# Four moves at the changeover of a two-layer block: the last chunk's root, the first routing weights' transposes, the shared expert's slice, and GpSimd's first product

## The reference

```python
xn = _layernorm(x)
x = x + L1_attn(xn) + L1_ffn(xn)
# L1_attn: q, k, v of the same token; for each token position a softmax over the 8 batch entries
attn = softmax(einsum('nqd,nkd->nqk', q, k) * scale)
out = einsum('nqk,nkd->nqd', attn, v) @ out_w.T + out_b
# L1_ffn: 16 experts of width 64, and a shared one of width 128
scores = sigmoid(x @ w_gate.T)
# groups of 4 experts; the 2 groups with the highest sum of their 2 best; then the 4 best experts
w = top4 / (sum(top4) + 1e-06)
combine = one_hot(idx) * w
routed = sum over e of combine[e] * (silu(x @ w1[e].T) * (x @ w3[e].T)) @ w2[e].T
shared = (silu(x @ w1_s.T) * (x @ w3_s.T)) @ w2_s.T
```

## Time and profile before

| | |
|---|---|
| median of 3 runs | 369.76 us (369.0 to 370.84) |
| profiled execution | 369.26 us |
| its span | 367.4 us |
| VectorE busy | 316.3 us, 86% |
| TensorE busy | 304.5 us, 83% |
| GpSimd busy | 238.8 us, 65% |
| ScalarE busy | 186.2 us, 51% |

### The profile page before, as it was taken

One profiled execution on the slowest core, in us unless ns is written; L12 is line 12 of the kernel. 1 busy time (PEld: TensorE's weight loads), 2 busy tenths in 40 slices (PEclk: granted clock), 3 DMA queues, 4 the chain that ended last, 5 costly groups with the idle time before them and its releaser, 6 DMA issues.

```text
span 367.4 us, 4905 instructions
## 1 busy us (share of the span) xinstructions
PE 304.5 (83%) x1371; PEld 218.4 (59%) x1371; DVE 316.3 (86%) x828; ACT 186.2 (51%) x505; POOL 238.8 (65%) x152
## 2 busy tenths in 40 slices
PE   0559777989889876773998988999999999899994
PEld 0336655868768665652654665765656666575662
DVE  5997899987987859837999999899898989989792
ACT  3346676866878586570253523635335362353611
POOL 3176487573745720142789679889898898988661
PEclk9978999999999999697999999999999999999999
DMA  4690000000000000008843324434333253324000
GB/s 137 176 271 1 2 0 1 3 1 2 1 1 2 0 1 2 0 14 160 186 113 57 96 79 101 100 87 129 110 91 117 58 140 87 115 83 118 3 29 29
DMA packets 21311, 24.81 MB, mean 68 GB/s; under 512 B 2428, under 2 KB 12068, under 8 KB 21284
## 3 DMA queue, kind: packets, MB, share of 16 engines
q1 hardware_dynamic: 20336, 24.09, 25.2%
q10 hardware_dynamic: 820, 0.39, 0.4%
q0 software_dynamic: 128, 0.01, 0.0%
HBM read 22.13 MB, written 2.36 MB: 67 GB/s over the span
## 4 chain that ended last, share of the span: by engine, by line
DVE 37%; PE 30%; issue 12%; POOL 8%; ACT 7%; DMA 3%; SPq 1%; ACTq 0%; DVEq 0%; POOLq 0%
PE Q L901 13%; PE VN L901 8%; PE T L901 5%; POOL prod_qk L841 5%; DVE att L1529 4%; DVE hid L1566 4%; DVE sgc L1553 3%; DVE rope_b L1305 3%; DVE rope_a L1303 3%; PE T L897 3%; POOL prod_pv L851 2%; DVE attn L1335 2%; ACT L735 1%; DVE xT_lo L1356 1%; DMA cw<-comb_table 1%
## 5 line engine op out<-in xcount | busy, mean ns | idle before, releaser
L841 POOL TENSOR_TENSOR prod_qk<-qkv 128x1024 f32<-128x1024 f32 x32 | 76.1, 2389 | 21.6 <-ACT qkv L551 12.4
L851 POOL TENSOR_TENSOR prod_pv<-prob,qkv 128x1024 f32<-128x1024 f32 x32 | 69.4, 2187 | 16.7 <-DVE att L1529 15.1
L901 PE MATMUL VN<-hid,w 128*128 128x512 f32 x144 | 74.6, 599 | 0.9 <-DVE hid L1566 0.9
L901 PE MATMUL Q<-xT_hi,w_hi 128*128 128x512 f32 x72 | 52.0, 722 | 1.2 <-issue 0.7
L1566 DVE TENSOR_TENSOR hid<-T,sgc 128x512 f32<-128x512 f32 x64 | 43.5, 680 | 0.0
L1515 DVE TENSOR_REDUCE scr<-prod_qk 128x128 f32<-128x1024 f32 x32 | 38.8, 1213 | 4.5 <-POOL prod_qk L841 4.3
L901 PE MATMUL Q<-bias,ones 128*128 128x400 f32 (+1 forms) x64 | 29.4, 459 | 15.2 <-ACT v_ext L629 7.1
L901 PE MATMUL T<-xT_hi,w_hi 128*128 128x512 f32 x72 | 30.5, 424 | 13.1 <-DVE hid L1566 13.0
L735 ACT ACTIVATE VN<-Q 128x512 f32<-128x512 f32 x32 | 18.6, 582 | 40.1 <-PE Q L901 26.5
L1529 DVE TENSOR_REDUCE att<-prod_pv 128x128 f32<-128x1024 f32 x32 | 38.3, 1198 | 0.0
L735 ACT ACTIVATE ND<-Q 128x512 f32<-128x512 f32 x32 | 18.6, 582 | 35.1 <-PE Q L901 32.2
(11 more groups left out here) (173 smaller groups left out, 761.8 us busy)
## 6 DMA issues: line engine op xcount, KB each, us to landing
cw<-comb_table SPq DMA_DIRECT2D x64, 256.0 KB, 4.5
out_x<-fin SPq DMA_DIRECT2D x8, 256.0 KB, 4.5
x<-in_x SPq DMA_DIRECT2D x2, 256.0 KB, 2.9
wraw<-in_w1T SPq DMA_DIRECT2D x1, 512.0 KB, 4.2
w3raw<-in_w3T SPq DMA_DIRECT2D x1, 512.0 KB, 4.7
w<-in_w2T SPq DMA_DIRECT2D x1, 512.0 KB, 5.8
rope_s<-in_c_sin ACTq DMA_DIRECT2D x1, 256.0 KB, 5.0
rope_c<-in_c_cos SPq DMA_DIRECT2D x1, 256.0 KB, 5.5
```

The costliest lines, as they stand in the source:

```text
L841: pool.tensor_tensor(prod_qk[:, t % 2], bc(qkv2[:, TH * half + t, j, 0:D], 1, NB), qkv2[:, :, j, D:2 * D], ALU.mult).then_inc(qk_prod, 1)
L851: pool.tensor_tensor(prod_pv[:, t % 2].rearrange("p (h e) b -> p b h e", e=HD), bc(prob[:, t].rearrange("p h b -> p b h"), 3, HD), qkv2[:, ...
L901: return pe.matmul(o, lhsT, rhs, start=start, stop=stop)
```

## The change

**The last chunk's root.** In step 9 the four layer-1 copies: ScalarE copies tile 0, and takes tiles 1 to 3 only behind the roots of step 10. The Sqrt table is loaded behind the copy `attnT` instead of ahead of it. VectorE's `route_masked` and `route_top` of half 0 move from step 9 to step 10, behind `plus_ffn`, and the first part of `route_chosen` behind `rms_values` of step 10.

**The first weights' transposes** stand ahead of chunk 7's tiles on TensorE, their copy ahead of the tiles' copies on ScalarE, followed by a two-element Sigmoid.

**Shared slice first.** The shared expert is slice 0 of each slot; routed slices are 1 to 8 (`routed_slice(s)` is s - 1, and w1, w3 and w2 are addressed by it). TensorE begins slot 0 when 31 of 32 tiles are kept.

**GpSimd's first product** waits until VectorE has done `route_above` of half 1 (`r_step` 16).

The diff:

```diff
--- before.py
+++ after.py
@@ -404,6 +404,8 @@
         NSLICE = NSLOT * NS
         BASE = (5, 14, 23, 31, 40, 48, 57, 65)
         LAST = BASE[NSLOT - 1] + 15
+        R_ROUTE = 13
+        R_ABOVE = R_ROUTE + 3
         COMB_AT = BASE[0] + 15
 
         def comb_bank(h):
@@ -413,6 +415,10 @@
 
 
             return (n + s) % 2
+
+        def routed_slice(s):
+
+            return s - 1
 
         def place(n):
 
@@ -660,6 +666,9 @@
                 if i == 1:
                     xnT_evac(0)
                 norms_rooted(i)
+                if i == STEPS - 2:
+                    for j in range(1, NJ):
+                        l1_tile(j)(i - 5)
                 if i == 3:
                     vu_norm()
                 if i > 1:
@@ -682,14 +691,17 @@
                 run(i, 4, xn2T_hi_evac)
                 if at(i, STEPS - 3):
                     sigmoid(0)
-                    act.activation(vu_n[:, 0, :], vu_n[:, 0, :], ACT.Sqrt)
                 run(i, 1, qkv_tile(2))
                 run(i, 2, attnT_evac)
+                if at(i, STEPS - 3):
+                    act.activation(vu_n[:, 0, :], vu_n[:, 0, :], ACT.Sqrt)
                 if i == STEPS - 2:
                     return
                 run(i, 1, qkv_tile(3))
                 run(i, 4, l1_tile(0))
                 run(i, 2, out_squares)
+                if i == STEPS - 3:
+                    return
                 run(i, 4, l1_tile(1))
                 run_end(i, 4, l1_tile(2))
                 run_end(i, 4, l1_tile(3))
@@ -712,11 +724,10 @@
                 l1_tile(2)(NB - 2)
                 l1_tile(3)(NB - 2)
                 xn2T_hi_evac(NB - 1)
-                l1_tile(0)(NB - 1)
-                l1_tile(1)(NB - 1)
                 combT_evac(0)
-                l1_tile(2)(NB - 1)
-                l1_tile(3)(NB - 1)
+                act.activation(vu_n[:, 0, :], vu_n[:, 0, :], ACT.Sigmoid)
+                for j in range(NJ):
+                    l1_tile(j)(NB - 1)
 
             pipeline(act, step, last_step)
 
@@ -727,11 +738,11 @@
             def gate(n, s):
                 act.wait_ge(g_ps, NS * n + s + 1)
 
-                if s >= 2:
-                    act.wait_ge(sgc_ready, (NS - 1) * n + s - 1)
+                if s >= 3:
+                    act.wait_ge(sgc_ready, (NS - 1) * n + s - 2)
                 else:
                     after(act, hid_ready, NS * n + s - 1)
-                gated = SB[side(n, s)] if s < NS - 1 else sg
+                gated = SB[side(n, s)] if s > 0 else sg
                 act.activation(gated[:, :], QB[side(n, s)][:, :], ACT.Silu).then_inc(sg_ready, 1)
 
             def attT_evac(u):
@@ -855,6 +866,7 @@
                         ALU.mult).then_inc(pv_prod, 1)
 
             pool.wait_ge(l1_kept, NT)
+            pool.wait_ge(r_step, R_ABOVE)
             for t in range(TH):
                 product_qk(0, t, 0, 0)
 
@@ -1039,12 +1051,12 @@
                 run(i, 1, qkv_tile(2))
                 run(i, 1, qkv_tile(3))
                 run(i, 2, attn_transposes(i))
+                if at(i, STEPS - 1):
+                    comb_transposes(0)
                 run(i, 2, ffn_product)
                 run(i, 4, l1_tile(0))
                 run(i, 2, output_product)
                 run(i, 4, l1_tile(1))
-                if at(i, STEPS - 1):
-                    comb_transposes(0)
                 run_end(i, 4, l1_tile(2))
                 run_end(i, 4, l1_tile(3))
                 if at(i, 1):
@@ -1058,7 +1070,7 @@
             pe.wait_ge(xn2T_lo, NB)
 
             pe.wait_ge(combT_ready, 1)
-            pe.wait_ge(l1_kept, NT)
+            pe.wait_ge(l1_kept, NT - 1)
             pe.wait_ge(w1_ready, 1)
             pe.wait_ge(w3_ready, 1)
             pe.wait_ge(ld_w2, 64)
@@ -1071,7 +1083,7 @@
                 pe.wait_ge(hid_ready, NS * n + s + 1)
                 if s == 0:
                     after(pe, yT_ready, n)
-                mm(VK[:, :], w2[:, s, :], hid[:, s % 3, :], s == 0, s == NS - 1).then_inc(y_ps, 1)
+                mm(VK[:, :], w2[:, routed_slice(s) % NS, :], hid[:, s % 3, :], s == 0, s == NS - 1).then_inc(y_ps, 1)
 
             def down_two_before(n, s):
 
@@ -1100,7 +1112,10 @@
                 j, half = place(n)
                 hi = xT_hi[:, TH * half:TH * half + TH, j, :]
                 lo = xT_lo[:, TH * half:TH * half + TH, j, :]
-                w = slice(s * P, (s + 1) * P)
+                at = routed_slice(s) % NS
+                w = slice(at * P, (at + 1) * P)
+                if n == 0 and s == 1:
+                    pe.wait_ge(l1_kept, NT)
 
                 after(pe, sg_ready, NS * n + s - 1)
                 g = QB[side(n, s)]
@@ -1398,6 +1413,8 @@
                     if g < NG - 1:
                         a = V.tensor_tensor(above[:, :, g, g + 1:NG], gv[:, :, g + 1:NG], own(NG - 1 - g), ALU.is_gt)
                 step_of(a)
+                if h == 1:
+                    assert r_done[0] == R_ABOVE
 
             def route_limits(h):
 
@@ -1472,7 +1489,8 @@
                 run(i, 2, head_blocks)
                 run(i, 3, plus_ffn)
                 if at(i, STEPS - 2):
-                    route_chosen(0, 0)
+                    route_masked(0)
+                    route_top(0)
                 if at(i, STEPS - 1):
                     route_chosen(0, 1)
                     route_weights(0)
@@ -1499,9 +1517,8 @@
                     route_limits(0)
                 if before_last(i):
                     rms_values(i)
-                if at(i, STEPS - 3):
-                    route_masked(0)
-                    route_top(0)
+                if at(i, STEPS - 2):
+                    route_chosen(0, 0)
                 if at(i, 1):
                     vu_sum()
 
@@ -1546,23 +1563,24 @@
 
             def weighted(n, s, k):
 
-                if s < NS - 1:
+                if s > 0:
+                    r = routed_slice(s)
                     dve.wait_ge(sg_ready, NS * n + s + 1)
-                    if s % 2 == 0:
-                        dve.wait_ge(ld_cw[s // 2], 32 * (n + 1))
-                    V.tensor_tensor(sgc[:, k, :], SB[k][:, :], cw[:, s // 2, s % 2, :], ALU.mult)\
+                    if r % 2 == 0:
+                        dve.wait_ge(ld_cw[r // 2], 32 * (n + 1))
+                    V.tensor_tensor(sgc[:, k, :], SB[k][:, :], cw[:, r // 2, r % 2, :], ALU.mult)\
                         .then_inc(sgc_ready, 1)
 
             def hidden(n, s, k):
 
-                if s < NS - 1:
-                    dve.wait_ge(sgc_ready, (NS - 1) * n + s + 1)
+                if s > 0:
+                    dve.wait_ge(sgc_ready, (NS - 1) * n + s)
                 else:
                     dve.wait_ge(sg_ready, NS * n + s + 1)
                 dve.wait_ge(u_ps, NS * n + s + 1)
 
                 after(dve, y_ps, NS * n + s - 2)
-                src = sgc[:, k, :] if s < NS - 1 else sg[:, :]
+                src = sgc[:, k, :] if s > 0 else sg[:, :]
                 V.tensor_tensor(hid[:, s % 3, :], UB[k][:, :], src, ALU.mult)\
                     .then_inc(hid_ready, 1)
```

## The result

The changed kernel takes 364.74 us (median of 4 runs, 364.25 to 365.62) against 369.69 us (4 runs, 369.00 to 370.84) for the kernel before on the same chip: ratio 0.9866, 95% interval 0.9834 to 0.9898, which is 4.95 us or 1.3% faster. Forecast: 365.1. Two of the later executions of the kernel before were far off (1048.70 and 1670.61 us) and are left out everywhere. The changed kernel's profiled execution took 365.62 us with a span of 363.8 us at a mean granted clock of 0.975.

A forecast was written before the change was run, and what follows sets the result against it. No engine bounds it throughout; VectorE's fixed list waits for the first weights' DMA and ScalarE's sigmoid. 5.01 + 0.35 + 0.28 - 0.65 - 0.60 = 4.4 us; span 363.0, execution 364.9, forecast 365.1 us; range 363.3 to 367.9.

The forecast's parts named there:

- The multiply of the second slice: Slot 0 on VectorE: begins at 166.73 instead of 171.74, waiting for the first weights; gain 5.01 us.
- Gate stalls: VectorE's idle before `sgc` at 177.07 and before 187.66, for late gates, goes: gain 0.35 and 0.28 us.
- Slot 4: GpSimd's fourth product waits for a later `att` sum without slack, delaying the next `scr`: about 0.65 us lost.
- rivals B: The late sum costs 0.60 us in every slot, not one: 368.5 us, no change; chance 0.1.
- D: Each slot's third gate waits for the first `hid`, stalling VectorE 1.07 us per slot: 371.8 us, slower; chance 0.03.
- The last slice: At the end VectorE is continuously busy, so one more multiply in the last slice costs 0.60 us in full.
- Roots: Steps 9 and 10 on VectorE: routing moved behind chunk 6's roots; last chunk's roots and `comb` gain under 0.1 us.
- before 165: Sign that the forecast is right: the first `hid` of slot 0, expected at about 163.8, begins before 165.
- a gain near 7: Weights' DMA estimated at 2.6 us for 256 KB: they land 3 us sooner, gain near 7 us.
- Rival C: Another release than the transfer comes last before slot 0's multiply: gain 1.5 to 3.5, about 366.7 us; chance 0.12.
- The clock: TensorE's new gap, from about 167 to 169.5, some 2.5 us: granted clock stays 1.00 from 160 to 180.
- Rival A: TensorE falls cold in its new gap, keeping the old 0.28 us stall: gain 3.5, 365.8 us; chance 0.2.

The follow-up runs named there:

- u_comb: Changed kernel with the routing weights' transposes and copy behind tile 1 of chunk 7 again: 368.28 us, ratio 0.9939.
- slot0: Changed kernel with the shared slice first in slot 0 only, last in the others: 364.48 us, repeated 364.24 us, ratio 0.984 and 0.9842.
- u_pool: Changed kernel without GpSimd's wait for the comparisons before its first product: 368.6 us, ratio 0.9936.
- u_shared: Changed kernel with the shared slice last in every slot again: 366.49 us, ratio 0.9892.
- late_pool: Changed kernel with GpSimd's first product waiting behind `limit` of half 1 too: 365.82 us, ratio 0.9891.
- slot0_late: Changed kernel with the shared slice first in slot 0 only and GpSimd's first product behind `limit` of half 1: 365.1 us, ratio 0.9864.
- u_root: Changed kernel with chunk 5's copies, the Sqrt load and half 0's masked/top/chosen at their old places: 364.81 us, ratio 0.9842.
- only_pool: Kernel before with only GpSimd's first product waiting for the comparisons of half 1: 370.24 us, ratio 1.0003.

## Why the prediction was right, and where it was off

**The sum.** Forecast 4.4 us in the trace, measured 4.85 (first profile) and 4.24 (second, 215.94 - 211.70). Time forecast 365.1, measured 364.74 and 365.19. Two sums of the prediction don't come out, and neither enters the forecast: a landing 3.8 us after its issue instead of 5.7 is 1.9 us sooner, not 1.3, and the times of the rivals leave out the 0.2 us that the forecast adds for the median.

**The multiply of the second slice, 5.01 us.** Measured 5.58 and 4.97, the spread being when the weights land. The copy was 3.47 us sooner against 3.25, the last release was the DMA, as written. u_comb shows this term by itself: without the early copy the multiply stands at 27.03, 3.2 to 3.8 us later, some of it by the half-speed tiles of that profile.

**Gate stalls, 0.35 + 0.28.** Both are gone in the changed kernel and in slot0; matched instruction by instruction, the lead grows by 0.71 us between the second slice's multiply and that of slice 7. In five kernels whose TensorE gap comes later against VectorE's list (u_comb, u_pool, u_shared, late_pool, slot0_late) VectorE waits for gates there again, 0.4 to 0.7 us.

**Slot 4, -0.65.** It came where it was put, 0.68 us at 289.34 behind GpSimd's late product; slot0 and u_shared remove it. The lead in the traces' own times (1.22 us less than from `root<-ss`) was 5.03 to 5.09 us through slots 1 to 3, 4.83 after a wait for a gate at 271.14 that I had not foreseen (0.24 us, gone in slot0), 4.25 at 289.34, and 4.23 at the start of the last slot's second slice. So no other slot lost anything: rivals B (0.60 in each) and D (1.07 in most) are out.

**The last slice, -0.60.** The lead at the last `hid` is 3.63 (4.85 from `root<-ss`), 0.60 less. The size was right and the reason wrong. I took it for a multiply pushed into the end of the kernel. If so, slot0, which ends on the shared slice, would have got it back, and it didn't: 187.13 is the old 187.15, less the 0.63 of stalls, plus 0.60. The multiply that is counted is slot 0's own first one. Before, it lay ahead of the instruction from which I measured; with the shared slice first it lies behind. Every order has the same multiplies after the weights land.

**Roots, "under 0.1 us" for `comb`.** Measured 0.30 against the profile before, and this was a lucky profile. In the old order TensorE idles 4.01 us before chunk 6's four transposes, and in three kernels with that order (and in u_root) they ran at 0.50 and took 1.11 us instead of 0.66. TensorE in order of time, of the kernel before:

```profile
147.75 0.66 PE L897 MATMUL T<-ident,xn 128*128 128x128 f32 x4 [4.01 <-ACT xn L588]
```

and of only_pool:

```profile
148.17 1.11 PE L898 MATMUL T<-ident,xn 128*128 128x128 f32 x4 [4.01 <-ACT xn L588]
```

`comb` is at 12.62 before and at 13.07 to 13.09 in those four, but at 12.32 to 12.35 in all nine profiles with the new order, although the transposes took anything from 0.65 to 1.12 us there: `masked` and `top` stand before `xT_lo` and cover it. So in the traces this part is worth 0.3 to 0.8 us at `comb`, and 1.5 us at the first `hid` (22.31 against 23.80 in u_root), since chunk 6's tiles begin sooner too; in the times it isn't seen (u_root 0.9842). only_pool, which by time changes nothing, has these slow transposes and a stretch of 216.49, so an ordinary execution of the kernel before may lie nearer to that than to 215.94; its one profile can't say.

**The step that was mis-sized: the slack of the VectorE path.** I had its first `hid` at 163.8, which leaves 2.3 us of cover before the weights. The first `hid` was at 165.26 in the old trace's time (142.95 + 22.31), so the sign "before 165" didn't hold, and the slack was 0.3 to 0.9 us. The prediction had named the reason as a possibility, with the first `hid` at 165.65: it cited the Trainium skill, "GPSIMD Engine Reference", Specifications, and said that `limit` beside the product might stretch to the product's end. It did, in every kernel where it ran beside the product (2.08 us), and not where the product starts behind it (0.20 us in late_pool). What that section of the Trainium skill names is two-port modes and instructions with two SBUF inputs. The trace agrees for `pairs`, which has two (0.33 us alone, 2.48 beside a product in u_pool); `limit` has one, and no run shows in which mode it ran.

This didn't move the total, as the prediction said. But it makes the low end of the range (363.3, by a sooner landing) unreachable: with the weights there at once the multiply could have begun only 0.3 to 0.9 us sooner. The same holds against the estimate of a gain near 7. It came from the Trainium skill, "DMA: Bandwidth & Descriptors", Anatomy of one DMA, whose fit is given for DMAs that GpSimd issues. The loads here are issued by SyncE and landed in 3.8 to 9.7 us (median 4.5) in the changed kernel too. And the slack decides what GpSimd's wait is worth. The expectation for u_pool had `pairs` at 3.5 us in all and the first `hid` 1.0 us later. It was 4.70 us (160.50 to 165.20) and 2.2, and the time 368.6 instead of 365.4. In u_root `comb` came 0.77 us later instead of 0.4 and the stretch grew by 1.17, but the time, 364.81, was the expected 365.0. Rival C's other release is what holds in these two, though not in the changed kernel.

**The clock.** Expected warm through the gap, and wrong: 0.50 near 170, as the list of signs against had it. Rival A's mechanism occurred, its price didn't. A stall appeared only where TensorE resumed later against VectorE's list (169.04 in late_pool, 26.39 us behind `root<-ss`, costs 0.65 us), not at 167.21, which is 23.04 behind it.

## What to carry to other kernels

Before pricing parts one by one, list every path that ends at the instruction whose start sets the rest, with its slack; a part on a path that is not last is worth nothing alone (only_pool, 1.0003) and something once the others are in (u_pool, 0.9936 against 0.9866). Take from a profile which wait releases what, and the price from the times of many executions: single profiles made the four parts cost 10.2 us, the times 5.4. Work that needs no late input should stand first only where something late is waited for: in slot 0 here, not in all eight. Count from an instruction ahead of the change, and profile the old order more than once, because its one profile may be a good one.

## What the runs showed of the hardware

- Beside a GpSimd product a VectorE instruction with one SBUF tensor as input stretched to the product's end: `limit`, 128 x 64, 0.20 to 2.08 us in each of the six profiles where it was beside one. With two SBUF inputs `pairs` went from 0.36 to 2.31 and from 0.33 to 2.48 us. The reduction `scr` took 1.21 us beside a product (167.99 in the changed kernel) and without one (172.34 before).
- A TensorE gap of 2.4 us with the clock at 1.00 all through it was followed by half speed for some 3 us after work had resumed, where a gap of 4.01 us left the transposes behind it at full speed in one profile and not in four others. In u_comb a gap of 1.41 us was followed by half speed from 157.8 to 161.0. The same program meets the clock in either state: chunk 6's transposes took 0.95 and 0.65 us in the two profiles of the changed kernel.
- The same transfer of weights, from the copy on ScalarE to the multiply that waits for it, took 9.9 to 10.6 us over the changed kernel, slot0 and u_comb. This is the spread of 0.6 us in the stretches.
